# Attention probabilities transposed in 64x64 quarters inside the scoring visits of a three-block decoder layer

## The chip, the cores and the metric

The kernel runs on one core of a Trainium2 chip. The metric is the time of one execution on the device in microseconds; less is better. The engines of the core work side by side, each through a list of its own: TensorE (PE: matmuls, with PEld for the load of their stationary operand), VectorE (DVE), ScalarE (ACT), GpSimd (POOL), and SyncE (SP), which here only issues transfers. They meet through semaphores.

## The reference, cut to what matters

Everything is float32. x is (4, 256, 512), the context (4, 64, 512). Each of three blocks is followed by a residual and a layer norm:

```python
attn = einsum('ds,td->st', w1, w2) * sparse_mask          # block 1, 512x512
x = layernorm(x + gelu(einsum('bds,st->bdt', x, attn) + b2))
q = rope(x @ wq)          # block 2: 32 query heads of 128
k = rope(ctx @ wk); v = ctx @ wv                          # 8 key/value heads of 128, 64 keys
p = softmax(q @ k.T / sqrt(128) + mask)                   # per head and batch: 256 x 64
x = layernorm(x + (p @ v) @ wo)
x = layernorm(x + x @ W.T + b + lora(x, routing))         # block 3, 8 experts of rank 16
```

## The kernel before, in words

The tokens are 1024 rows, in 8 tiles of 128 (t = 0..7). A product that must keep float32 quality is made of three matmuls on operands that are split into a high and a low part (`mm3`, lines 261 to 263: high by high, low by high, high by low). ACT copies the high part out of PSUM (all its copies are line 801), DVE subtracts it to get the low part (all such subtractions are line 1139).

Block 2 is a loop over the 8 key/value heads g (`LAST` = 7). Group 0 is begun ahead of the hardware loop, which runs six times (g = 1..6), and group 7 is written out behind it. A group has four units u = 0..3: half u//2 of the tokens (tiles 4\*(u//2) to 4\*(u//2)+3) and a pair u%2 of its four query heads. For each unit:

- `query` (PE): two projections f = 0, 1 of 12 matmuls of 512 columns; ACT copies (`q_copy`), DVE and POOL rotate (`q_cos`, `q_sin`, `q_rot`).
- `scores`, or `score_pair` for two units at once (PE, line 369): the array is used as four quarters of 64x64; a quarter is plain float32, and each such matmul of the code is two MATMUL records in the trace.
- softmax: `mask_scores`, `row_max`, `shift` (DVE), `exps` (ACT), `row_sum`, `row_inverse` (DVE), `probs` (POOL, line 1728), which leaves the probabilities in SM, 128 tokens by 8 times 64.
- `probs_transpose` (PE, line 393): four 128x128 transposes of SM against the identity ID into one PSUM bank; `pt_hi` (ACT) and `pt_lo` (DVE) take them to PTh and PTl.
- `value_out(g, n)` (PE, n = 0..7): the values times a head's rows of wo, evicted by `vw_hi` and `vw_lo` to VWh and VWl; `attend(g, t)` (PE): six matmuls for a token tile, PT times VW, which `accumulate` (DVE) adds to the residual X, a step counted by the semaphore `x_added`.

The order of each engine's list is written out by hand; so are the PSUM banks (`T_BANKS` of the transposes, `A_BANKS` of attend, the last argument of `value_out`). A bank must have been read before PE writes it again, and this is why many waits on `x_added`, `vw_lo` and `pt_lo` stand in PE's list. After the loop the norm of block 2 needs an inverse root, found by a chain of 12 small dependent steps on POOL (`newton`, lines 1707 to 1713) behind DVE's `stats` and `guess`; ahead of the loop it is the same for block 1.

Of the kernel before, what the change touches and what calls it, by code (L numbers as in the profile page):

```python
# [9 lines left out]
F32R = mybir.dt.float32r  # L10
# [21 lines left out]
def decoder_layer(nc, x, ctx_in, amask, w1, w2, b2, smask, wq, wk, wv, wo, fW, fb, fA, fB, rW, rb, rope, out):  # L32
# [24 lines left out]
    with ExitStack() as es:  # L57
# [24 lines left out]
        PTh, PTl = (sb(f"PT{s}", [P, 2, B * S], F32R) for s in "hl")  # L82
# [26 lines left out]
        T_BANKS, A_BANKS = (7, 6, 7, 6), (6, 3, 6, 6, 6, 6, 3, 6)  # L109
# [49 lines left out]
        def x2_bank(t):  # L159
            return (5, 4, 3, 4, 3, 5, 3, 5)[t]  # L160
# [18 lines left out]

        def s_tiles(u):  # L180
            at = u % 2 * 4 * KS
            return bank[:, S_BANK:S_BANK + 2, at:at + 4 * KS].rearrange("p a (t k) -> p a t k", k=KS)

        def fy_bank(t):
            return (0, 6, 2, 7, 1, 3, 6, 7)[t]
# [8 lines left out]
        F_BANKS = (3, 0, 2, 1, 2, 1, 2)  # L194
        LORA_BANKS, ROUTE_BANK = (4, 3), 5
        TR_BANKS, W2_BANKS, AT_BANK = (6, 7, 0, 1, 6, 7, 0, 1, 6, 7, 6, 7, 6, 7, 6, 7, 6, 7), (0, 1, 6, 7), 2
        X_AT = (0, 1, 2, 3, 5, 7, 8, 9)
        X1_AT = (10, 11, 12, 13, 14, 15, 16, 17)
# [59 lines left out]
        def _(pe):  # L258
# [58 lines left out]
            def dense(t):  # L317
# [4 lines left out]
                pe.matmul(o, PTh[:, 1, 0:P], PTh[:, 0, 0:D], start=True, stop=False)  # L322
# [12 lines left out]
            def keys(g):  # L335
                pe.wait_ge(sm["wkv_lo"], 2 * g + 1)
                if isinstance(g, int) and g == 0:
                    pe.wait_ge(sm["tr_lo"], 7)
                project(k_out(g), 0).then_inc(sm["k_mm"], 1)

            def values(g):
                pe.wait_ge(sm["wkv_lo"], 2 * g + 2)
                if isinstance(g, int) and g == 0:
                    pe.wait_ge(sm["tr_lo"], 7)
                project(v_out(g), 1).then_inc(sm["v_mm"], 1)
# [59 lines left out]
            def attend(g, t):  # L405
# [5 lines left out]
                for pair in range(2):  # L411
                    m = mm3(bank[:, A_BANKS[t], :], PTh[:, pair, t * P:(t + 1) * P], PTl[:, pair, t * P:(t + 1) * P],
# [36 lines left out]
            def lora_out(t):  # L449
                pe.wait_ge(sm["ts_lo"], t // 4 + 1)  # L450
                pe.wait_ge(sm["f_lo"], 6)
                mm3(bank[:, fy_bank(t), :], PTh[:, 0, t * P:(t + 1) * P], PTl[:, 0, t * P:(t + 1) * P],
# [20 lines left out]
            w2_transpose(3)  # L473
            attn_chunk(1)
            pe.wait_ge(sm["w2t_lo"], 3)
            x_tile(0, 0)
            pe.wait_ge(sm["w2t_lo"], 4)
# [3 lines left out]
            attn_chunk(2)  # L481
            attn_last(0)
            attn_last(1)
            attn_last(2)
            pe.wait_ge(sm["w2t_lo"], 2)
            x_tile(3, 3)
            attn_last(3)
            pe.wait_ge(sm["tr_lo"], 1)
            ctx_tile(0, 4)
            pe.wait_ge(sm["tr_lo"], 2)  # L490
            x_tile(4, 5)
            pe.wait_ge(sm["tr_lo"], 3)
            ctx_tile(1, 6)
            pe.wait_ge(sm["tr_lo"], 4)
            x_tile(5, 7)
            pe.wait_ge(sm["at_masked"], 1)
            dense(0)
            pe.wait_ge(sm["at_masked"], 2)
# [30 lines left out]
            query(0, 0, 0)  # L529
            pe.wait_ge(sm["tr_lo"], 14)  # L530
            value_out(0, 0, 7)
            pe.wait_ge(sm["x_added"], 7)
            query(0, 0, 1)
            pe.wait_ge(sm["tr_lo"], 13)
            x1_tile(4, 14)
            pe.wait_ge(sm["x_added"], 8)
            value_out(0, 1, 3)
            pe.wait_ge(sm["vw_lo"], n_vw(0, 0))
            x1_tile(5, 15)
# [4 lines left out]
            pe.wait_ge(sm["at_masked"], 3)  # L544
            pe.wait_ge(sm["at_masked"], 4)
            scores(0, 0)
            pe.wait_ge(sm["tr_lo"], 15)
            x1_tile(6, 16)
            pe.wait_ge(sm["tr_lo"], 16)
            x1_tile(7, 17)  # L550
            pe.wait_ge(sm["q_rot"], n_rot(0, 0, 1))
            query(0, 1, 1)
            pe.wait_ge(sm["k_cos"], 1 + 1)
            query(0, 2, 0)
            pe.wait_ge(sm["tr_lo"], 18)
            value_out(0, 2, 7)
            pe.wait_ge(sm["vw_lo"], n_vw(0, 1))
            value_out(0, 3, 3)
# [3 lines left out]
            probs_transpose(0, 0)  # L562
            pe.wait_ge(sm["q_rot"], n_rot(0, 1, 0))
            query(0, 3, 0)
            pe.wait_ge(sm["vw_lo"], n_vw(0, 3))
# [3 lines left out]
            pe.wait_ge(sm["s_sub"], n_unit(0, 0))  # L569
            scores(0, 1)  # L570
            pe.wait_ge(sm["pt_lo"], n_unit(0, 0))
            value_out(0, 5, 7)

            with pe.Fori(1, LAST) as g:
                pe.wait_ge(sm["k_cos"], g + 1)
                query(g, 0, 0)
                pe.wait_ge(sm["s_sub"], n_unit(g - 1, 1))
                score_pair(g - 1, 3)
                pe.wait_ge(sm["q_rot"], n_rot(g - 1, 3, 0))
                values(g)  # L580
                pe.wait_ge(sm["x_added"], n_added(g - 2, 7))
                probs_transpose(g - 1, 1)
                pe.wait_ge(sm["vw_lo"], n_vw(g - 1, 4))
                value_out(g - 1, 6, 3)
                pe.wait_ge(sm["q_rot"], n_rot(g - 1, 3, 1))
                query(g, 0, 1)
                pe.wait_ge(sm["pt_lo"], n_unit(g - 1, 1))
                attend(g - 1, 0)
                pe.wait_ge(sm["vw_lo"], n_vw(g - 1, 5))
                value_out(g - 1, 7, 7)  # L590
                pe.wait_ge(sm["vw_lo"], n_vw(g - 1, 6))
                attend(g - 1, 1)
# [3 lines left out]
                probs_transpose(g - 1, 2)  # L596
                pe.wait_ge(sm["q_rot"], n_rot(g, 0, 1))
                query(g, 1, 1)
                pe.wait_ge(sm["pt_lo"], n_unit(g - 1, 2))
                value_out(g, 0, 7)  # L600
                pe.wait_ge(sm["x_added"], n_added(g - 1, 0))
                attend(g - 1, 2)
# [3 lines left out]
                attend(g - 1, 3)  # L606
                pe.wait_ge(sm["s_sub"], n_unit(g - 1, 3))
                score_pair(g, 1)
                pe.wait_ge(sm["x_added"], n_added(g - 1, 3))
                probs_transpose(g - 1, 3)  # L610
                pe.wait_ge(sm["x_added"], n_added(g - 1, 1))
                value_out(g, 1, 3)
                pe.wait_ge(sm["q_rot"], n_rot(g, 1, 1))
                query(g, 2, 1)
                pe.wait_ge(sm["pt_lo"], n_unit(g - 1, 3))
                attend(g - 1, 4)
                pe.wait_ge(sm["q_rot"], n_rot(g, 1, 0))
                query(g, 3, 0)
                pe.wait_ge(sm["vw_lo"], n_vw(g, 0))
                value_out(g, 2, 7)  # L620
                pe.wait_ge(sm["q_rot"], n_rot(g, 2, 0))
                keys(g + 1)
                pe.wait_ge(sm["vw_lo"], n_vw(g, 1))
                value_out(g, 3, 3)
                pe.wait_ge(sm["x_added"], n_added(g - 1, 4))
                attend(g - 1, 5)
                pe.wait_ge(sm["vw_lo"], n_vw(g, 2))
                probs_transpose(g, 0)
                pe.wait_ge(sm["q_rot"], n_rot(g, 2, 1))
                query(g, 3, 1)  # L630
                pe.wait_ge(sm["vw_lo"], n_vw(g, 3))
                attend(g - 1, 6)
                pe.wait_ge(sm["x_added"], n_added(g - 1, 5))
                attend(g - 1, 7)
                pe.wait_ge(sm["x_added"], n_added(g - 1, 6))
                value_out(g, 4, 3)
                pe.wait_ge(sm["pt_lo"], n_unit(g, 0))
                value_out(g, 5, 7)

            pe.wait_ge(sm["k_cos"], LAST + 1)  # L640
            query(LAST, 0, 0)
            pe.wait_ge(sm["vw_lo"], n_vw(LAST - 1, 4))
            value_out(LAST - 1, 6, 3)
            pe.wait_ge(sm["x_added"], n_added(5, 7))
            probs_transpose(LAST - 1, 1)
# [1257 lines left out]
```

## Time and profile before

| what | value |
|---|---|
| time, median of 3 runs | 492.2 us (491.89 to 492.32) |
| profiled execution, time | 492.99 us |
| its span, first to last instruction | 491.2 us |
| PE busy | 473.9 us, 96% |
| DVE / ACT / POOL busy | 408.3 / 260.6 / 273.4 us |
| mean granted clock of TensorE | 0.985 |

The span is what the trace shows; the profiled execution's own time is 1.8 us longer, for what lies around it. Matmuls overlap, so the share of PE is no measure of its speed, but a stretch in which PE never waits is one in which only less or cheaper PE work, or more clock, makes the kernel shorter.

### The profile page before, as it was taken

The numbers are of one execution on the slowest core, as the hardware profiler recorded it, in microseconds if no ns is written. First come the engines' busy times: TensorE is split into PE (matmuls) and PEld (weight loads), VectorE is DVE, ScalarE is ACT, GpSimd is POOL, SyncE is SP. The second block draws the span as 40 slices with busy tenths as digits, with TensorE's granted clock in tenths as the row PEclk, the third lists the DMA queues.
The fourth block names the chain that finished last, engine by engine and source line by source line (L and its number), as shares of the span: only waits on it lengthen the run. The fifth ranks groups of instructions, "written<-read, shape, count | busy, mean of one in ns | idle before, by whom it ended". The sixth has DMA issues, their size and how long they took to land.

```text
span 491.2 us, 11126 instructions
## 1 busy us (share of the span) xinstructions
PE 473.9 (96%) x4189; PEld 395.9 (81%) x4189; DVE 408.3 (83%) x739; ACT 260.6 (53%) x462; POOL 273.4 (56%) x347
## 2 busy tenths in 40 slices
PE   8999999999999999999999999999999999879991
PEld 8888778888888888888888888888888788668781
DVE  2779898988987898798979987988799889988585
ACT  4574447735673566365735663575458254353423
POOL 3477637854674467456636672676366423156523
PEclk9999999999999999999999999999999999979996
DMA  8943300240023011402040212022002400000013
GB/s 274 353 146 93 124 1 1 87 130 1 2 85 128 0 22 63 128 0 80 7 127 0 85 34 94 0 85 85 0 0 87 67 1 2 1 0 2 0 40 133
DMA packets 29137, 31.56 MB, mean 64 GB/s; under 512 B 6321, under 2 KB 16817, under 8 KB 29114
## 3 DMA queue, kind: packets, MB, share of 16 engines
q1 hardware_dynamic: 29114, 31.25, 20.1%
q8 instruction: 15, 0.25, 0.2%
q14 instruction: 8, 0.07, 0.0%
HBM read 29.15 MB, written 2.10 MB: 64 GB/s over the span
## 4 chain that ended last, share of the span: by engine, by line
PE 77%; DVE 9%; SPq 4%; POOL 3%; issue 3%; DMA 2%; ACT 1%; ACTq 0%; POOLq 0%; DVEq 0%
PE bank L261 23%; PE bank L263 22%; PE bank L262 22%; PE bank L369 6%; PE bank L393 3%; SPq L205 2%; DMA WQr<-in_L_xattn_wq_dram 2%; DVE X L1223 1%; DVE BST L1187 1%; PE bank L267 1%; POOL NW L1711 1%; DVE VWl L1139 1%; POOL NW L1709 1%; POOL RS L1713 1%; POOL NW L1707 1%
## 5 line engine op out<-in xcount | busy, mean ns | idle before, releaser
L1722 POOL TENSOR_TENSOR QS<-QS,SIN 128x512 f32<-128x512 f32 x64 | 83.0, 1297 | 124.4 <-ACT QS L801 124.4
L261 PE MATMUL bank<-XTh,WQh 128*128 128x512 f32 x256 | 101.7, 397 | 0.7 <-DVE XTl L1139 0.7
L263 PE MATMUL bank<-XTh,WQl 128*128 128x512 f32 x256 | 100.0, 391 | 0.0
L262 PE MATMUL bank<-XTl,WQh 128*128 128x512 f32 x256 | 99.7, 390 | 0.0
L1139 DVE TENSOR_TENSOR VWl<-bank,VWh 64x512 fp32r<-64x512 f32 x128 | 88.0, 688 | 9.3 <-ACT VWh L801 7.4
L801 ACT ACTIVATE QS<-bank 128x512 f32<-128x512 f32 x64 | 38.3, 598 | 103.1 <-PE bank L263 102.6
L801 ACT ACTIVATE VWh<-bank 64x512 fp32r<-64x512 f32 x128 | 75.9, 593 | 23.5 <-PE bank L263 20.9
L1251 DVE TENSOR_TENSOR bank<-bank,COS 128x512 f32<-128x512 f32 x64 | 44.6, 697 | 23.2 <-ACT QS L801 22.6
L261 PEld LDWEIGHTS bank<-XTh,WQh 128*128 128x128 f32 x256 | 48.1, 188 | 11.5 <-issue 1.3
L263 PEld LDWEIGHTS bank<-XTh,WQl 128*128 128x128 f32 x256 | 48.0, 188 | 10.5
L262 PEld LDWEIGHTS bank<-XTl,WQh 128*128 128x128 f32 x256 | 48.1, 188 | 9.5
L261 PE MATMUL bank<-VWh,PTh 128*128 128x512 f32 x128 | 50.9, 398 | 0.4 <-DVE X L1314 0.3
L262 PE MATMUL bank<-VWl,PTh 128*128 128x512 f32 x128 | 50.3, 393 | 0.0
L263 PE MATMUL bank<-VWh,PTl 128*128 128x512 f32 x128 | 50.1, 392 | 0.0
L1314 DVE TENSOR_TENSOR X<-X,bank 128x512 f32<-128x512 f32 x64 | 43.2, 674 | 7.2 <-PE bank L263 6.3
L1698 POOL TENSOR_TENSOR WOl<-WOr,WOh 128x512 fp32r<-128x512 f32 x32 | 41.3, 1291 | 12.1 <-ACT WOh L801 11.6
L1263 DVE TENSOR_TENSOR QR<-bank,QS 128x512 f32<-128x512 f32 x64 | 42.9, 683 | 0.4
L1688 POOL TENSOR_TENSOR WQl<-WQr,WQh 128x512 fp32r<-128x512 f32 x32 | 41.0, 1304 | 2.1 <-ACT WQh L801 2.1
L369 PEld LDWEIGHTS bank<-KK,QR 64*64 64x64 f32 x2048 | 31.6, 135 | 5.9 <-issue 5.8
L1728 POOL TENSOR_TENSOR SM<-SM,RI 128x512 f32<-128x512 f32 x32 | 33.5, 1046 | 3.8 <-DVE RI L1296 3.8
L369 PE MATMUL bank<-KK,QR 64*64 64x64 f32 x2048 | 34.2, 220 | 0.0
L261 PEld LDWEIGHTS bank<-VWh,PTh 128*128 128x128 f32 x128 | 24.3, 190 | 6.0 <-DVE X L1314 1.0
(150 smaller groups left out, 965.1 us busy)
## 6 DMA issues: line engine op xcount, KB each, us to landing
WQr<-in_L_xattn_wq_dram SPq DMA_DIRECT2D x8, 1024.0 KB, 5.5
WOr<-in_L_xattn_wo_dram SPq DMA_DIRECT2D x8, 1024.0 KB, 5.4
KVr<-in_L_xattn_wk_dram SPq DMA_DIRECT2D x8, 256.0 KB, 5.4
KVr<-in_L_xattn_wv_dram SPq DMA_DIRECT2D x8, 256.0 KB, 5.5
out_dram<-X SPq DMA_DIRECT2D x8, 256.0 KB, 2.0
X<-in_x_dram SPq DMA_DIRECT2D x3, 512.0 KB, 9.9
WQr<-in_L_attn_w_dram SPq DMA_DIRECT2D x4, 256.0 KB, 4.9
WOr<-in_L_attn_w_dram SPq DMA_DIRECT2D x4, 256.0 KB, 5.1
```

Of the source, the lines that this page charges most:

```text
L261: pe.matmul(o, lh, rh, start=start, stop=False)
L262: pe.matmul(o, lh, rl, start=False, stop=False)
L263: return pe.matmul(o, ll, rh, start=False, stop=stop)
L369: m = pe.matmul(s_tiles(u)[part, a, t, :], QR[head, u % 2, f, t * P + part.start:t * P + part.stop], KK[head, b, f, :], start=f == 0, stop ...
L801: return act.activation(o, i, ACT.Copy)
L1139: return dve.tensor_tensor(o, i, f32(hi), ALU.subtract)
L1251: dve.tensor_tensor(q, q, by_pos(COS, 2, S), ALU.mult).then_inc(sm["q_cos"], 1)
L1263: dve.tensor_tensor(QR[:, u % 2, f, :], bank[:, q_bank(u, f), :], QS[:, u % 2, 1 - f, :], ALU.add if f else ALU.subtract).then_inc(sm["q_r ...
L1314: dve.tensor_tensor(X[:, t, :], X[:, t, :], bank[:, A_BANKS[t], :], ALU.add)\
L1688: pool.tensor_tensor(wq_split(WQl, h), wq_head(WQr, h), f32(wq_split(WQh, h)), ALU.subtract)\
L1698: pool.tensor_tensor(WOl[:, h, :], WOr[:, h, :], f32(WOh[:, h, :]), ALU.subtract)\
L1722: pool.tensor_tensor(q, q, SIN[:, :].unsqueeze(1).broadcast_to([P, 2, S]), ALU.mult)\
```

## The change

1. `score_pair`, the visit that scores two units, first transposes the probabilities of the two units before them: `pair_transposes` issues 32 matmuls of 64x64 quarters (four for each 128x128 block of SM, each a plain float32 matmul of a piece of SM with a 64x64 piece of the identity) into the banks 6 and 7. `probs_transpose` stays only for the last two units of group 6 and the four of group 7.
2. One ACT copy (`pt_hi_pair`) and one DVE subtraction (`pt_lo_pair`) of 1024 columns over both banks take the place of two of each of 512. PTh and PTl are laid out anew for it (half, pair, 512).
3. `score_pair` now waits for the probabilities of both units (`p_done`) and for both banks, ahead of the scoring too.
4. The lists of all engines are written in another order, in all three stages, and many banks are others. One `value_out` of a group (n = 5) goes from the end of a loop pass to the start of the next.

```diff
+            def pair_transposes():
+                for n in range(8):
+                    for q in range(4):
+                        r, key = slice(64 * (q % 2), 64 * (q % 2) + 64), slice(64 * (q // 2), 64 * (q // 2) + 64)
+                        m = pe.matmul(t_quads()[key, q % 2, n, :], SM[r, n // 4, n % 4 * P + key.start:n % 4 * P + key.stop], ID[r, r],
+                                      start=True, stop=True)
+                return m
...
             def score_pair(g, u):
+                pe.wait_ge(sm["p_done"], UNITS * g + u - 1)
                 pe.wait_ge(sm["q_rot"], 2 * UNITS * g + 2 * u + 2)
...
                 pe.sem_inc(sm["s_begun"], 1)
+                pair_transposes().then_inc(sm["t_mm"], 2)
                 unit_scores(u - 1)
                 unit_scores(u).then_inc(sm["s_mm"], 2)
...
+            def pt_hi_pair(g, u):
+                act.wait_ge(sm["t_mm"], UNITS * g + u + 1)
+                if counted(g):
+                    act.wait_ge(sm["x_added"], n_added(g - 1, 2 * u + 1))
+                copy(pt_quads(PTh, u // 2), t_quads()).then_inc(sm["pt_hi"], 2)
...
+            def pt_lo_pair(g, u):
+                dve.wait_ge(sm["pt_hi"], UNITS * g + u + 1)
+                lo_part(pt_quads(PTl, u // 2), t_quads(), pt_quads(PTh, u // 2)).then_inc(sm["pt_lo"], 2)
...
-        T_BANKS, A_BANKS = (7, 6, 7, 6), (6, 3, 6, 6, 6, 6, 3, 6)
+        T_BANK = 6
+        T_BANKS, A_BANKS = (7, 7, 7, 7), (7, 6, 6, 7, 6, 3, 7, 6)
```

PE, in the loop, at the scoring visit of units 0 and 1 of group g. Before, the quarters of the scores stand alone, and a transposing visit (ID, SM) follows:

```order
L369 MATMUL bank<-KK,QR 64x64 x64
L609 REGISTER_ALU
L393 MATMUL bank<-ID,SM 128x128 x4
L611 REGISTER_ALU
L261 MATMUL bank<-WOh,VTh 128x512
```

After, at the same visit:

```order
L388 MATMUL bank<-ID,SM 64x64 x32
L379 MATMUL bank<-KK,QR 64x64 x64
L632 REGISTER_ALU
L271 MATMUL bank<-WOh,VTh 128x512
L272 MATMUL bank<-WOl,VTh 128x512
```

The transposes went from behind the scores to ahead of them, became 32 quarters for two units, and one such entry serves where two x4 entries were in a loop pass.

DVE, in the loop, behind the scoring visit of units 2 and 3 of the group before (KK,QR of PE). Before:

```order
L1280 TENSOR_REDUCE MX<-bank 128x8
L1275 SCALAR_TENSOR_TENSOR bank<-bank,MSK 128x2x256
L1285 REGISTER_ALU
L1287 TENSOR_TENSOR SM<-bank,MX 128x2x4x64
L1299 REGISTER_ALU
L1139 TENSOR_TENSOR PTl<-bank,PTh 128x512
```

After:

```order
L1290 SCALAR_TENSOR_TENSOR bank<-bank,MSK 128x2x256
L1294 REGISTER_ALU
L1295 TENSOR_REDUCE MX<-bank 128x8
L1154 TENSOR_TENSOR PTl<-bank,PTh 128x2x8x64
L1278 TENSOR_TENSOR QR<-bank,QS 128x512
```

The subtraction for PTl is one of twice the size, third behind the mask and the maximum of unit 2.

POOL, behind the loop, where group 7 ends. Before, the end of the first Newton chain, its shift, the last unit's `probs` and the first `add_bias`:

```order
L1711 TENSOR_SCALAR NW<-NW 128x2
L1713 TENSOR_TENSOR RS<-RS,NW 128x2
L1758 TENSOR_TENSOR NM<-MV,RS 128x2
L1760 TENSOR_SCALAR NM<-NM 128x2
L1728 TENSOR_TENSOR SM<-SM,RI 128x512
L1765 TENSOR_TENSOR X<-X,WOr 128x512 x2
```

After, the `probs` of the last units and the begin of that chain:

```order
L1738 TENSOR_TENSOR QS<-QS,SIN 128x512 x2
L1744 TENSOR_TENSOR SM<-SM,RI 128x512 x2
L1723 TENSOR_TENSOR NW<-RS 128x2
L1725 TENSOR_TENSOR NW<-NW,VH 128x2
L1727 TENSOR_SCALAR NW<-NW 128x2
```

The last unit's `probs` stood behind the whole chain and its shift, and now stands ahead of it.

## Rows read from the trace of the kernel before

**Rows 1.** The page's head: the span, and the busy time of each engine.

```profile
span 491.2 us, 11126 instructions
PE 473.9 (96%) x4189; PEld 395.9 (81%) x4189; DVE 408.3 (83%) x739; ACT 260.6 (53%) x462; POOL 273.4 (56%) x347
```

**Rows 2.** Windows: length, then PE, PEld, DVE, ACT, POOL busy; clock, DMA, GB/s.

```profile
228.10:275.40 47.30, 47.30 (x466) 39.72 (x465) 40.48 (x67) 26.60 (x49) 28.41 (x25) 1.00 0.18 55
370.00:437.00 67.00, 62.59 (x652) 51.80 (x650) 61.19 (x110) 34.73 (x62) 27.25 (x36) 0.97 0.12 29
```

**Rows 3.** The page's chain that ended last, by engine.

```profile
PE 77%; DVE 9%; SPq 4%; POOL 3%; issue 3%; DMA 2%; ACT 1%; ACTq 0%; POOLq 0%; DVEq 0%
```

**Rows 4.** Timeline of PE: first query of loop, of group 7, last matmul.

```profile
86.34 0.39 PE L261 MATMUL bank<-XTh,WQh 128*128 128x512 f32 x1
...
370.03 0.39 PE L261 MATMUL bank<-XTh,WQh 128*128 128x512 f32 x1
...
480.65 0.39 PE L263 MATMUL bank<-WOh,PTl 128*128 128x512 f32 x1
```

**Rows 5.** Groups of PE by form: records, busy us, mean ns.

```profile
L369 PE MATMUL bank<-KK,QR 64*64 64x64 f32 x2048 | 34.2, 220 | 0.0
L393 PE MATMUL bank<-ID,SM 128*128 128x128 f32 x128 | 19.9, 280 | 2.3 <-POOL SM L1728 2.3
L282 PE MATMUL bank<-ID 128*128 128x128 f32 x24 | 4.7, 371 | 1.5 <-POOL ID L1769 1.5
```

**Rows 6.** Timeline of PE around one transposing visit of the loop.

```profile
220.65 0.39 PE L263 MATMUL bank<-VWh,PTl 128*128 128x512 f32 x1
220.88 0.60 PE L393 MATMUL bank<-ID,SM 128*128 128x128 f32 x4
221.23 0.48 PE L261 MATMUL bank<-XTh,WQh 128*128 128x512 f32 x1
221.55 0.40 PE L262 MATMUL bank<-XTl,WQh 128*128 128x512 f32 x1
```

**Rows 7.** Timeline of PE: a scoring visit of one unit, one of two.

```profile
84.45 1.16 PE L369 MATMUL bank<-KK,QR 64*64 64x64 f32 x64
85.54 0.50 PE L261 MATMUL bank<-WOh,VTh 128*128 128x512 f32 x1
...
230.98 2.10 PE L369 MATMUL bank<-KK,QR 64*64 64x64 f32 x128
233.00 0.39 PE L261 MATMUL bank<-CTh,KVh 128*128 128x256 f32 x1
```

**Rows 8.** Timeline of DVE in the loop: PTl; mask and maximum behind the scores.

```profile
223.31 0.68 DVE L1139 TENSOR_TENSOR PTl<-bank,PTh 128x512 fp32r<-128x512 f32 x1
...
233.14 0.70 DVE L1275 SCALAR_TENSOR_TENSOR bank<-bank,MSK 128x512 f32<-128x512 f32 x1 [0.36 <-PE bank L369]
233.87 0.69 DVE L1280 TENSOR_REDUCE MX<-bank 128x8 f32<-128x512 f32 x1
```

**Rows 9.** Timeline of ACT in the loop: a copy of 1024 columns.

```profile
234.86 1.06 ACT L801 ACTIVATE KVh<-KVr 128x1024 fp32r<-128x1024 f32 x1
```

**Rows 10.** Timeline of PE ahead of the loop: the longest wait there.

```profile
53.30 0.47 PE L261 MATMUL bank<-XTh,WQh 128*128 128x512 f32 x1 [0.65 <-DVE XTl L1139]
```

**Rows 11.** Timeline of PE in group 7: its two long waits.

```profile
429.93 0.50 PE L261 MATMUL bank<-WOh,VTh 128*128 128x512 f32 x1 [1.69 <-DVE VWl L1139]
...
433.63 1.08 PE L393 MATMUL bank<-ID,SM 128*128 128x128 f32 x4 [2.30 <-POOL SM L1728]
```

**Rows 12.** Timeline of POOL in group 7: first step of the chain, last `probs`.

```profile
428.53 0.19 POOL L1707 TENSOR_TENSOR NW<-RS 128x2 f32<-128x2 f32 x1 [8.15 <-DVE RS L1203]
...
432.44 1.04 POOL L1728 TENSOR_TENSOR SM<-SM,RI 128x512 f32<-128x512 f32 x1
```

**Rows 13.** Windows of 5 us in group 7, columns as in Rows 2.

```profile
430.00:435.00 5.00, 2.70 (x14) 2.31 (x15) 4.84 (x10) 4.13 (x8) 2.75 (x10) 0.74 0.00 0
435.00:440.00 5.00, 5.00 (x20) 4.38 (x19) 3.21 (x7) 2.14 (x4) 2.51 (x2) 0.58 0.00 0
```

More of the change, by code:

```diff
@@ L605, in _ @@
                 pe.wait_ge(sm["x_added"], n_added(g - 1, 2))
[L606 to L612, printed above, removed]
+                value_out(g, 1, 6)
+                pe.wait_ge(sm["vw_lo"], n_vw(g, 0))
+                value_out(g, 2, 3)
@@ L679, in _ @@
+            query(LAST, 2, 1)
+            pe.wait_ge(sm["pt_lo"], n_unit(LAST - 1, 3))
             probs_transpose(LAST, 0)
-            pe.wait_ge(sm["vw_lo"], n_vw(LAST, 0))
-            value_out(LAST, 1, 3)
-            pe.wait_ge(sm["x_added"], n_added(LAST - 1, 3))
+            pe.wait_ge(sm["q_rot"], n_rot(LAST, 1, 0))
+            weight_transpose(1)
+            pe.wait_ge(sm["vw_lo"], n_vw(LAST, 1))
             attend(LAST - 1, 4)
+            pe.wait_ge(sm["f_lo"], 1)
+            attend(LAST - 1, 5)
@@ L720, in _ @@
+            pe.wait_ge(sm["x_added"], n_added(LAST - 1, 7))
+            attend(LAST, 1)
+            pe.wait_ge(sm["x_added"], n_added(LAST, 1))
+            attend(LAST, 2)
+            pe.wait_ge(sm["x_added"], n_added(LAST, 0))
+            probs_transpose(LAST, 2)
+            pe.wait_ge(sm["q_rot"], n_rot(LAST, 2, 0))
+            weight_transpose(3)
+            pe.wait_ge(sm["vw_lo"], n_vw(LAST, 4))
+            value_out(LAST, 5, 3)
             pe.wait_ge(sm["x_added"], n_added(LAST, 2))
+            value_out(LAST, 6, 6)
@@ new lines, in _ @@
+            pe.wait_ge(sm["vw_lo"], n_vw(LAST, 6))
+            attend(LAST, 4)
+            pe.wait_ge(sm["vw_lo"], n_vw(LAST, 7))
+            attend(LAST, 5)
+            pe.wait_ge(sm["pt_lo"], n_unit(LAST, 3))
+            attend(LAST, 6)
+            pe.wait_ge(sm["x_added"], n_added(LAST, 4))
+            attend(LAST, 7)
+            pe.wait_ge(sm["tr_lo"], 19)
+            x2_tile(1)
+            pe.wait_ge(sm["f_lo"], 4)
+            base(0)
+            pe.wait_ge(sm["s_sub"], n_unit(LAST, 3))
@@ L1551, in _ @@
+            vw_lo(LAST - 1, 7, 3)
+            q_cos(LAST, 0, 1)
+            v_lo(LAST)
+            q_rot(LAST, 0, 0)
             mask_scores(LAST - 1, 2)
+            pt_lo_pair(LAST - 1, 1)
+            q_rot(LAST, 0, 1)
             row_max(LAST - 1, 2)
@@ L1579, in _ @@
+            q_rot(LAST, 1, 1)
+            row_max(LAST, 0)
+            accumulate(LAST - 1, 3)
+            vw_lo(LAST, 0, 3)
+            shift(LAST, 0)
+            q_cos(LAST, 2, 0)
+            row_sum(LAST, 0)
+            pt_lo(LAST - 1, 3)
             row_inverse(LAST, 0)
-            q_rot(LAST, 1, 1)
-            vw_lo(LAST, 0, 3)
-            q_cos(LAST, 2, 0)
+            vw_lo(LAST, 1, 6)
             mask_scores(LAST, 1)
             row_max(LAST, 1)
+            shift(LAST, 1)
@@ L1625, in _ @@
-            f_lo(2)
-            row_inverse(LAST, 3)
-            vw_lo(LAST, 6, 3)
+            accumulate(LAST - 1, 6)
+            q_rot(LAST, 3, 0)
+            accumulate(LAST - 1, 7)
+            q_rot(LAST, 3, 1)
+            f_lo(2)
+            accumulate(LAST, 0)
+            stats(1, 0)
+            mask_scores(LAST, 3)
+            row_max(LAST, 3)
+            vw_lo(LAST, 4, 3)
+            accumulate(LAST, 1)
+            shift(LAST, 3)
+            stats(1, 1)
+            row_sum(LAST, 3)
@@ L1628, in _ @@
+            accumulate(LAST, 2)
+            row_inverse(LAST, 3)
+            pt_lo(LAST, 2)
+            guess(1, 0)
+            f_lo(3)
+            vw_lo(LAST, 5, 3)
+            accumulate(LAST, 3)
+            vw_lo(LAST, 6, 6)
             stats(1, 2)
[L1629 to L1630 removed]
             pt_lo(LAST, 3)
+            stats(1, 3)
+            vw_lo(LAST, 7, 3)
+            guess(1, 1)
             x2_lo(0)
[L1633 removed]
             accumulate(LAST, 4)
[L1635 removed]
```

819 lines of the change are left out of this document (378 added, 441 removed).

## The prediction

> **What bounds the kernel now.** I read the page's head and the chain first. PE is busy for 96% of the span [rows 1], and 77% of the chain that ended last is PE [rows 3]. The share says little while matmuls overlap, so I looked at where PE waits. A window of one loop pass is 47.30 us long with PE busy for all 47.30 and the clock at 1.00 [rows 2]: in the loop PE never waits. There only the price of PE's own work counts, and any delay of another engine is free up to its slack. The window of group 7 has 62.6 of 67.0 us busy and a clock of 0.97 [rows 2]: here waits and the clock decide, and DVE, busy for 61.2, sets them. From the first query of the loop to the first query of group 7 there are (370.03 - 86.34)/6 = 47.28 us a pass; ahead of the loop lie 86.3 us, behind it 121.1 us, of which PE works until about 480.9 [rows 4].
>
> **The transposes, the core of the change.** A transposing visit of PE stands between two matmuls that would follow each other at 0.23 us (220.65 to 220.88). From 220.65 to 221.55 are 0.90 us with one visit and two such steps, so the visit costs 0.44 us [rows 6], and two units 0.88.
>
> The new one is 32 matmuls of 64x64 quarters in plain float32. The program scores with 1024 such matmuls (32 for each of 32 units) and the trace has 2048 records of them; the 12 plain matmuls of the warming have 24 [rows 5]. The transposes that go have one record each, 128 for 32 units times 4 [rows 5]. So the 32 new matmuls are 64 records, not 32, and this decides the sum. A visit of 64 records takes 1.09 us until the next matmul, one of 128 takes 2.02 [rows 7]: 64 more records in a visit that is there anyway cost 0.93 us. They have the form of the scores (64 rows, 64 columns, the four quarters in turn, row halves to different banks), so I take 0.93; half of 2.02, 1.01, is the upper end, 0.46 the lower, if the trace's doubling did not hold here.
>
> A pair thus costs 0.93 for 0.88: +0.05. Against this stands that the matmuls right behind a lone transposing visit start a little apart (0.32 us for the first step, 0.23 otherwise, in [rows 6]), a few hundredths of which the 0.44 may miss. A pass has two pairs, and I take its PE work as unchanged, 47.28 us; from -0.15 to +0.25 a pass, which is -0.9 to +1.5 for six.
>
> A rule that speaks against the change: the Trainium skill (TensorEngine Tiling (Array Packing), Feature Incompatibilities) says that tiling by columns excludes the transpose mode for float32 inputs, and TensorE: Matmul & The Clock Gate (Terms) calls that mode four times faster for float32. By the whole of that factor the price of the eight blocks, 0.88 us, would be 3.5, halved for 64 instead of 128 columns 1.8 us a pair. By the row it is 0.93, since the scores already are plain quarters; the doubled records agree with the rule's direction, not with its size.
>
> **Evictions in the loop.** Two copies and two subtractions of 512 columns become one each of 1024. ACT has a copy of 1024 at 1.06 us [rows 9]. DVE's of 512 is 0.68 alone [rows 8] and follows another at about 0.6, so I take 1.25 for the pair (2 x 0.60 to 2 x 0.68). What counts is whether they are there in time, since nothing else waits on PE in a pass. Behind the visit of units 2 and 3, `pt_lo_pair` is third on DVE: the mask starts 0.14 after the visit (233.00, 233.14), the maximum 0.73 after the mask [rows 7, 8], the subtraction 0.6 later, and it ends 2.7 us behind the visit. PE has a query (12 x 0.227 = 2.7) and a `value_out` (0.7) to do, 3.4 us, ahead of `attend`, and wants the weights some 0.2 sooner. Slack 0.45 us. Behind the other visit it is one rotation (0.6), the mask (0.7) and the pair (1.25), again 2.7 against 3.4. The copy is ahead of both, since the transposes now stand ahead of the scores and end about 2 us before them. The probabilities are wanted ahead of the visit: POOL ends those of unit 1 about 1.2 us early, those of unit 3 about 0.8. So the loop has no wait, cost 0.
>
> **Ahead of the loop.** One `value_out` (3 x 0.23 = 0.68 us) and the visit of unit (0, 0), 0.44, leave it: -1.1. Its waits: now there is 0.8 us at 53.30 (52.49 to 53.30, of which the row calls 0.65 idle) [rows 10] and some 0.7 in two short ones. In the new order `x_tile(7)` waits for the copy and split of `x1_tile(1)`, which stands on DVE behind `normalize(0, 2)` and so behind the second Newton chain on POOL; the first chain is now behind one more subtraction of 1.3 us. I get PE ready at 45.1 and the tile at 46.6, a wait of 1.5, and 0.5 at the last quarter of `dense(0)`. New 2.0 for old 1.5: in sum -0.6, between -1.3 and +0.6.
>
> **Behind the loop.** The `value_out` comes here (+0.68), the pair of group 6 costs 0.93 for a 0.44 visit (+0.5). Before, PE waits 1.69 and 2.30 us [rows 11] and about 0.7 elsewhere. The second is there because the last `probs` stands behind the Newton chain and shift on POOL, from 428.53 to 432.44 [rows 12]. Then the clock falls to its half level, 1.2 GHz: windows at 0.74 and 0.58 make (0.26 + 0.42) x 5/0.5 = 6.8 us of it [rows 13], some 5.6 of them with PE at work, so 2.8 us lost. The transposes at 433.63 take 1.08 for 0.60 [rows 11, 6]. Together 7.5 us.
>
> After: `probs(7, 3)` stands ahead of the chain and that wait is gone, but others come. (a) `attend(7, 2)` follows `attend(7, 1)` in the same bank and waits for its `accumulate`, on DVE behind a mask, a maximum and a `vw_lo`: 1.9 us. (b) The transposes of (7, 3) wait for `accumulate(7, 3)`: 1.8. (c) `x2_tile(0)` waits for the first `normalize`, ACT behind the same 3.9 us of POOL chain and behind `vw_hi(7, 7)`: 1.7. (d) `attend(7, 4)` waits for the last `vw_lo`: 0.7. Together 6.2 us with the clock full: -1.3. At the very end POOL's last chains set the pace; `guess(2, 1)` comes some 0.6 us earlier against PE's end, so does the end: -0.7. The stage: +0.7 +0.5 -1.3 -0.7 = -0.8; with my walk's ends -2.5 to +1.0 at full clock.
>
> **Sum.** -0.6 + 0 - 0.8 = -1.4 us in the span of 491.2 [rows 1], 489.8. The profiled execution took 492.99 for it, the median of the runs 492.2; I apply the difference to the median: 490.8.
>
> **The rivals.**
> 1. *The clock halves again behind the loop.* For it: waits (b), (c), (d) stand within 7 us, 4.2 idle, while before 4.0 idle within 6 us went with the fall [rows 11, 13]; the total of the waits is larger. Against: single waits are shorter, the longest 1.9 for 2.30. PE then has some 5 us of bound work at half speed: +2.6, 493.4.
> 2. *The loop waits for the pair* (slower). DVE's list is full, and one subtraction of twice the size holds what is behind it. If `pt_lo_pair` ends over 0.45 us later than worked out, PE waits in each of six passes; at 1.2 us late in one place 6 x 0.75 = 4.5 us, 495.3. It decides from 0.6 us late on. Against: all durations are from rows, and there is no wait in the passes of before.
> 3. *The quarters are as dear as the rule on the transpose mode says*: 1.8 for 0.93 in 13 pairs, +11, 502. Against: 2048 records of that form at 0.93 for 64 [rows 5, 7].
> 4. *Better than summed*: the quarters are single records (0.46 each pair, 13 x -0.47 = -6, 484.7), or, likelier, waits (a) to (c) overlap with one another and the tail saves 3: 488.
> 5. *Nothing gained or lost*: the DVE and ACT time saved lies where PE never waits, and waits only change places. This is my sum without the tail's two gains, 492.
>
> **How the numbers follow.** Forecast 490.8 with 0.38 (its own range 489.7 to 492). Rival 1 0.25, rival 2 0.10, rival 3 0.03, rival 4 0.15, rival 5 0.09. A measurement of this kernel tells about 0.2%, 1.0 us, from no change. Below 491.2: 0.26 of the forecast's 0.38, all of 4, a little of 5: 0.43. Above 493.2: most of 1, 2 and 3: 0.28. Between: 0.29. The range leaves out 4's single records, the far side of 2, and 3: 487.8 to 494.6.
>
> **What the changed profile would show.** Right: 64 records of ID,SM quarters a pair at 14 to 16 ns apart; a pass between 47.1 and 47.5 us with PE busy throughout; the two 1024-column evictions at about 1.06 and 1.25 us; PE's first long wait at `x_tile(7)`; behind the loop waits at the second `attend` of group 7, at the last transposes, at the first `x2_tile`; no or a shorter window below clock 1.00 before PE's end. Wrong: a wait of PE for PTl in the passes (rival 2), 32 records or another spacing (3, 4), a window near 0.6 around the last transposes (1). If the stage ahead of the loop or behind it differs from my sum by over 1 us, the order was misread, not the price of the quarters.

## The result, and the profile after

| | before | after |
|---|---|---|
| median of runs, one chip | 492.26 us (491.89 to 493.34, 4 runs) | 497.77 us (497.05 to 498.36, 4 runs) |
| ratio, 95% interval | | 1.0107 (1.0092 to 1.0121) |
| span of the profiled execution | 491.2 us | 495.9 us |
| first query of the loop | 86.34 | 86.69 |
| one loop pass | 47.28 | 47.37 |
| first query of group 7 to the end | 121.2 | 125.0 |

The changed kernel is slower by 5.5 us, forecast was 1.4 less. Run again on another chip it took 498.01 us for 492.33, ratio 1.0099 (1.0084 to 1.0113). The spans differ by 4.7 us only, since the profiled execution of before was 0.7 above its median. One execution of experiment 9 (1215.81 us) is counted as slow and stays out of its ratio. The page's head, to be held against [rows 1]:

```profile
span 495.9 us, 12575 instructions
PE 474.7 (96%) x4917; PEld 397.1 (80%) x4917; DVE 411.7 (83%) x726; ACT 260.2 (52%) x449; POOL 272.6 (55%) x347
```

Windows of a loop pass and of two stretches of group 7, against [rows 2, 13], columns as there:

```profile
228.80:276.17 47.37, 47.37 (x577) 40.03 (x576) 40.21 (x65) 26.54 (x47) 28.29 (x25) 1.00 0.18 55
425.00:430.00 5.00, 2.94 (x13) 2.06 (x12) 4.82 (x10) 1.82 (x3) 0.00 (x0) 0.96 0.00 0
430.00:435.00 5.00, 5.00 (x21) 4.24 (x20) 3.38 (x11) 2.55 (x5) 1.94 (x6) 0.70 0.00 0
```

The reader sees again a pass without a wait, with 111 more records, and a stretch of 3.4 us at the half clock, (0.04 + 0.30) x 5/0.5, where before had 6.8. A pair's visit in the loop, timeline of PE, and the two evictions, of ACT and DVE:

```profile
237.52 0.39 PE L273 MATMUL bank<-XTh,WQl 128*128 128x512 f32 x1
237.84 1.16 PE L388 MATMUL bank<-ID,SM 64*64 64x64 f32 x64
238.82 2.05 PE L379 MATMUL bank<-KK,QR 64*64 64x64 f32 x128
240.80 0.50 PE L271 MATMUL bank<-XTh,WQh 128*128 128x512 f32 x1
...
239.78 1.02 ACT L813 ACTIVATE PTh<-bank 128x1024 fp32r<-128x1024 f32 x1
...
242.28 1.22 DVE L1154 TENSOR_TENSOR PTl<-bank,PTh 128x1024 fp32r<-128x1024 f32 x1
```

64 records and 0.98 us until the scores. The subtraction ends at 243.50, 2.7 us behind the visit as worked out. PE's list waits for it ahead of `attend`, whose first matmul starts at 244.34, so 0.84 us were to spare. All rows of the view of PE's waits (columns: us in total, times, longest):

```profile
PE bank L271 <- DVE X L1333: 2.1, 1, 2.1
PE bank L277 <- ACT X L944: 2.0, 2, 1.8
PE bank L277 <- DVE XTl L1154: 1.8, 1, 1.8
PE bank L292 <- POOL ID L1785: 1.5, 1, 1.5
PE bank L379 <- issue: 1.4, 1, 1.4
PE bank L414 <- DVE X L1333: 1.4, 1, 1.4
PE bank L271 <- DVE VWl L1154: 1.1, 2, 0.6
```

`x_tile`, `x1_tile` and `x2_tile` are the transposes of a token tile for blocks 1, 2 and 3, and `dense` is block 1's product. Five waits were forecast by place, and come within half a microsecond of their size: `x_tile(7)` ahead of the loop (1.5 forecast, 1.8), the second `attend` of group 7 (1.9, 2.1), the last transposes (1.8, 1.4), the first `x2_tile` (1.7, 1.8), `attend(7,4)` (0.7, 0.5). The row of ID stands in before too [rows 5]. One row, `issue`, is no wait for an engine and was not forecast. Timeline of PE at the only pair visit behind the loop:

```profile
379.93 1.16 PE L388 MATMUL bank<-ID,SM 64*64 64x64 f32 x64
380.91 1.79 PE L379 MATMUL bank<-KK,QR 64*64 64x64 f32 x107
384.13 0.57 PE L379 MATMUL bank<-KK,QR 64*64 64x64 f32 x21 [1.42 <-issue]
384.63 0.50 PE L271 MATMUL bank<-XTh,WQh 128*128 128x512 f32 x1
```

In the middle of the scores, with no semaphore between them, PE stands still for 1.42 us. The scores take 3.72 us (380.91 to 384.63) where in the loop they take 1.98, so the place costs 1.74. In the DMA view the queue of kind "instruction" has packets of 16 KB. Its rows for 130:369 (five passes, no q8) and for 380.5:383 (queue, kind: packets, MB, share):

```profile
q1 hardware_dynamic: 9504, 12.58, 16.6%
q14 instruction: 1, 0.01, 0.0%
...
q8 instruction: 1, 0.02, 2.4%
```

From 125.0 to 381.3 no packet of q8 comes, and the first one falls into this visit. Before has the same picture: none from 127 to 375.4, the first at 375.5, inside a visit with only 128 quarter records (373.96 to 375.99), and there PE does not stop.

**Where the span's 4.7 us are.** Ahead of the loop +0.35. The loop 6 x 0.09 = +0.55. Behind it +3.8. For this last part I added up in both traces what each step of PE takes over its plain cadence (0.227 us for a matmul of 512 columns, 0.119 for 256, 0.0155 for a quarter's record, 0.057 for a 128x128 transpose). The moved `value_out` is +0.68, the pair for a single visit +0.54, the stop in the scores +1.74, the other steps up to the scores of unit (7, 3) -0.6; from there to the four last `attend` 9.9 us over cadence for 9.0, +0.9; in block 3, where `x2_tile` now stands singly, 3.9 for 2.9, +1.0; the end behind PE's last matmul -0.5 (10.04 for 10.55 us).

### The profile page after: what moved, and what is told of

Its sections match the earlier page's. It is cut to its first block, busy times and chain, and to the rows that moved or that the text cites. A ratio compares the mean times of both kernels' runs of the same rounds, so it can differ in the third digit from the quotient of the medians.

```text
span 495.9 us, 12575 instructions
## 1 busy us (share of the span) xinstructions
PE 474.7 (96%) x4917; PEld 397.1 (80%) x4917; DVE 411.7 (83%) x726; ACT 260.2 (52%) x449; POOL 272.6 (55%) x347
## 4 chain that ended last, share of the span: by engine, by line
PE 84%; DVE 8%; POOL 3%; ACT 3%; issue 2%; POOLq 0%; ACTq 0%; DVEq 0%
PE bank L271 24%; PE bank L273 23%; PE bank L272 23%; PE bank L379 6%; PE bank L388 3%; DVE BST L1202 1%; PE bank L277 1%; DVE VWl L1154 1%; PE bank L292 1%; DVE X L1333 1%; DVE VE L1211 1%; POOL NW L1727 1%; ACT VWh L813 1%; POOL NW L1723 1%; DVE X L1238 1%
## 5 line engine op out<-in xcount | busy, mean ns | idle before, releaser
L909 ACT ACTIVATE SM<-SM 128x512 f32<-128x512 f32 x32 | 20.2, 631 | 43.6 <-DVE SM L1302 43.4
```

## The experiments

Times are medians beside the kernel before on the same chip (492.3 to 492.6 us in all); 497.8 and 498.0 are the changed kernel (ratios 1.0107 and 1.0099). Chips differ a little, so two versions on different chips are better compared by their ratios to the kernel before. The order of the first four follows one question: what is the stop inside the scores, and what does a pair cost?

**1. Whole transposes in the pair behind the loop (e1_whole_tail).**

In `score_pair`, where g is a number and not the loop's register (behind the loop), with evictions to match:

```diff
+            def whole_transposes():
+
+                for n in range(8):
+                    m = pe.transpose(bank[:, T_BANK + n // 4, n % 4 * P:(n % 4 + 1) * P], SM[:, n // 4, n % 4 * P:(n % 4 + 1) * P], ID[:, :])
+                return m
...
-                pair_transposes().then_inc(sm["t_mm"], 2)
+                (whole_transposes if isinstance(g, int) else pair_transposes)().then_inc(sm["t_mm"], 2)
```

> The changed kernel, but the one pair visit behind the loop (group 6, units 2 and 3) transposes with 8 whole 128x128 transposes, one record each, and not with 64 quarter records; the loop is untouched. Theory 'code supply': the gap of 1.42 us inside the scores of that visit is PE waiting for its own code, because 192 short records follow each other just where code has to be fetched again for the first time after the loop. With 136 records instead, the first fetch falls late in the scores, a long query follows, and the gap is gone: the visit (380.91 to 384.63 for the scores, 3.72 us) falls to about 2.0, the time by 1.5 to 1.8 us. Rival 'the pair itself' (the wait for both units, the banks, a transfer beside it): the gap stays at 1.2 to 1.6 us, the time changes by 0.1 or less.

495.88 us, ratio 1.0070 (1.0057 to 1.0084): 1.9 to 2.1 less than the changed kernel, 1.4 to 1.8 by the ratios. Timeline of PE at the visit:

```profile
379.39 1.04 PE L386 MATMUL bank<-ID,SM 128*128 128x128 f32 x8
380.36 2.10 PE L379 MATMUL bank<-KK,QR 64*64 64x64 f32 x128
382.38 0.50 PE L271 MATMUL bank<-XTh,WQh 128*128 128x512 f32 x1
```

The stop is gone and the scores take 2.02. From the first query of group 7 to PE's last matmul are 113.06 us (370.48 to 483.54) for 114.93.

**2. The stop made in the kernel before (e4_before_dense).**

In `score_pair` of the kernel before, again where g is a number:

```diff
+                if isinstance(g, int):
+                    unit_scores(u - 1)
                 unit_scores(u - 1)
                 unit_scores(u).then_inc(sm["s_mm"], 2)
```

> The kernel before with one thing added: in the double scoring visit behind the loop (group 6) the scores of one unit are issued twice (64 more quarter records, same result), so that the visit has 192 quarter records as the changed kernel has. Theory 'code supply': besides their own 0.99 us they bring a gap of about 1.0 to 1.7 us into that visit, in sum 2.0 to 2.7 us more. Rival 'the pair itself': 1.0 us more and no gap.

494.12 us, 1.0033 (1.0021 to 1.0045), so 1.5 more. Timeline of PE, the last of 192 quarter records (the first starts at 373.99) and what follows:

```profile
377.89 0.56 PE L369 MATMUL bank<-KK,QR 64*64 64x64 f32 x19 [1.12 <-issue]
378.38 0.38 PE L261 MATMUL bank<-CTh,KVh 128*128 128x256 f32 x1
```

The stop is there, without pair, new banks or new order. The scores take 4.39 us for 2.03, 2.4 more, as expected. The last transposes are 1.9 us late, and 0.9 of it came back since 3.4 us of group 7 then lay at the half clock for 6.8, which the expectation had left out. The rival (1.0 us and no stop) is refuted.

**3. The pair of the loop issued twice (e3_twice_loop).**

```diff
                 pe.sem_inc(sm["s_begun"], 1)
+                if not isinstance(g, int):
+                    pair_transposes()
                 pair_transposes().then_inc(sm["t_mm"], 2)
```

> The changed kernel with the pair transposes of the loop issued twice, the second time over the first (same result), so 12 more visits of 64 records. If a loop pass has no wait and a pair costs what its records show (0.98 us), a pass grows by 1.96 us and the time by 11.8. If the records hide a price or a slack is used up (evictions come 1 us later against the work that wants them only if that is ahead of the scores, so this is not expected), more than 13. If the pair overlaps with something, under 10.

511.66 us, 1.0396 (1.0380 to 1.0412): 13.9 more than the first measurement of the changed kernel, not 11.8. A pass from the second on is 49.24 us, 1.87 more for two pairs of visits: 0.93 each. The first pass is 2.7 us longer than the others (51.97). Timeline of PE in that pass:

```profile
97.95 2.03 PE L379 MATMUL bank<-KK,QR 64*64 64x64 f32 x123
101.34 0.34 PE L379 MATMUL bank<-KK,QR 64*64 64x64 f32 x5 [1.37 <-issue]
...
122.11 0.68 PE L379 MATMUL bank<-KK,QR 64*64 64x64 f32 x33
123.54 1.62 PE L379 MATMUL bank<-KK,QR 64*64 64x64 f32 x95 [0.75 <-issue]
```

So the stop comes with runs of many short records in code that runs for the first time, in the first pass and behind the loop (0.97 us here), and in none of the five repeated passes, though they have the same visits. That is what the supply of code would do, and nothing else proposed would. One thing more speaks for it: in all ten stops of the eight profiles that have one, PE goes on 2.2 to 2.7 us after a 16 KB packet of q8 has started (381.7 and 384.13 in the changed kernel, 375.5 and 377.89 in experiment 2). Not each such run stops, though: the changed kernel's first pass has two visits of 192 records (scores at 96.70 and 118.25), each with a packet of q8 in it, and no stop. What decides this, no run shows.

**4. All pairs whole (e2_whole_all).** The edit of 1 for every g.

> The changed kernel with all 13 pair visits made of 8 whole transposes. Theory 'priced by the row': an x8 visit of the kernel before takes 0.97 us until the scores behind it, the quarters take 0.98, and the step ahead of quarters is 0.32 for 0.23: 0.1 us less a pair, so a loop pass of 47.37 becomes about 47.17 and the loop 1.2 us shorter, with the 1.6 us behind the loop together 2.8 us less. Rival 'quarters are dear' (1.8 us a pair): over 10 us less. Rival 'quarters are free': a pass stays at 47.37 or gets longer.

497.0 us, 1.0084 (1.0071 to 1.0098), where 2.8 us less than the changed kernel, 495.0, was expected; the runs lie from 493.76 at a mean clock of 0.995 to 497.22 at 0.986, so the median says little. The profile decides the loop: a pass is 47.26, 0.12 less than with quarters and 0.02 less than before. A pair of quarters costs 0.06 us more than 8 whole transposes (0.1 was expected). They are neither dear nor free.

**5. The joined eviction split again (e5_split_evict).**

```diff
-                copy(pt_quads(PTh, u // 2), t_quads()).then_inc(sm["pt_hi"], 2)
+                for a in range(2):
+                    copy(w_unit(PTh, u // 2, a), t_unit(a)).then_inc(sm["pt_hi"], 1)
...
-                lo_part(pt_quads(PTl, u // 2), t_quads(), pt_quads(PTh, u // 2)).then_inc(sm["pt_lo"], 2)
+                for a in range(2):
+                    lo_part(w_unit(PTl, u // 2, a), t_unit(a), w_unit(PTh, u // 2, a)).then_inc(sm["pt_lo"], 1)
```

> The changed kernel, but each pair is evicted in two copies and two subtractions of 512 columns again (same banks, same quarters, same places in the lists of ScalarE and VectorE). A copy of 512 takes 0.60 us and two follow at about 0.5 to 0.6, so 1.1 for 1.02; two subtractions 1.3 for 1.22. Theory 'TensorE sets the loop': a pass stays at 47.37 us and the time at that of the changed kernel within 0.3 us; the joined eviction brought nothing. Rival 'VectorE's list is at its edge in the loop': each pair comes 0.1 to 0.2 us later and passes grow, by 1 us or more in all.

498.39 us, 1.0119 (1.0105 to 1.0134), 0.4 to 0.6 more (0.6 to 1.0 by the ratios). A pass is 47.37 us as in the changed kernel: in the loop the join brings nothing, as theory had it. The profiled execution was the longest of the five, 501.28 us, and its time went elsewhere. Timeline of PE ahead of the loop:

```profile
48.37 0.98 PE L283 MATMUL bank<-ID,X 128*128 128x128 f32 x4 [1.80 <-DVE XTl L1161]
49.00 0.78 PE L338 MATMUL bank<-PTh 128*128 128x512 f32 x1
49.57 0.63 PE L277 MATMUL bank<-VWh,XTh 128*128 128x512 f32 x1
```

Windows of the same kernel there:

```profile
45.00:50.00 5.00, 3.20 (x21) 2.81 (x19) 4.40 (x8) 1.75 (x5) 2.91 (x6) 0.86 0.20 59
50.00:55.00 5.00, 5.00 (x23) 4.16 (x22) 2.84 (x7) 3.39 (x7) 3.89 (x12) 0.80 0.47 181
```

Behind the same wait for `x_tile(7)`, 1.80 us, the granted clock is at its half level for (0.14 + 0.20) x 5/0.5 = 3.4 us, and the loop begins at 88.7 for 86.7. Group 7 of this profile has two more such stretches. What the other four executions lost, no trace shows.

**6. One wait behind the loop mended (e6_drain_swap, e7_bank0).** The first:

```diff
             row_max(LAST, 3)
-            vw_lo(LAST, 4, 3)
             accumulate(LAST, 1)
+            vw_lo(LAST, 4, 3)
```

> The changed kernel with two neighbours in VectorE's list of group 7 exchanged: accumulate of tile 1 stands ahead of the vw_lo of value_out 4. The second attend of group 7 waits 2.06 us for that accumulate (425.8 to 428.6). Theory 'each wait is one entry in a list': the wait shrinks by the 1.4 us of vw_lo, and what comes behind wants nothing earlier, so the time falls by 0.7 to 1.4 us, up to 3 if the clock does not fall behind the shorter wait. Rival 'VectorE as a whole sets the drain': the next wait grows by as much, and the time changes by less than 0.3.

498.11 us, 1.0108 (1.0095 to 1.0121): no gain. The profiled run was the longest, 498.93 us, and its clock fell ahead of the loop too (as in 5). Behind the loop its PE needs 114.12 us for 114.93. Rows of PE's waits in timeline form:

```profile
429.37 0.50 PE L271 MATMUL bank<-VWh,PTh 128*128 128x512 f32 x1 [0.78 <-DVE X L1333]
433.37 0.50 PE L271 MATMUL bank<-WOh,VTh 128*128 128x512 f32 x1 [0.78 <-DVE X L1333]
437.84 1.12 PE L414 MATMUL bank<-ID,SM 128*128 128x128 f32 x4 [2.12 <-DVE X L1333]
```

The wait went from 2.06 to 0.78; a new one of 0.78 stands at a `value_out`, and the next grew from 1.39 to 2.12. The second gives the last transposes bank 0:

```diff
-            pe.wait_ge(sm["x_added"], n_added(LAST, 3))
+            pe.wait_ge(sm["f_lo"], 4)
             probs_transpose(LAST, 3)
```

> The changed kernel with the transposes of the last unit of group 7 written to bank 0 and not 7, so that they wait for the weight split that last read bank 0 and not for the accumulate of tile 3 (1.39 us at 437.00). They should stand at 435.5. Theory 'each wait is one entry in a list': the last value_out then starts at 436.3 for 437.4, the copy of the probabilities and the first normalize on ScalarE come 1.1 to 1.5 us earlier, the wait at the first x2_tile goes from 440.5 to about 439.3, and the time falls by about 1.1. Rival 'VectorE as a whole sets the drain': under 0.3.

497.73 us, 1.0113 (1.0088 to 1.0138): nothing. The steps came where they were forecast, `value_out` at 436.28 and `x2_tile` at 439.46, and yet:

```profile
436.28 0.50 PE L274 MATMUL bank<-WOh,VTh 128*128 128x512 f32 x1 [0.21 <-DVE VWl L1157]
439.46 0.63 PE L280 MATMUL bank<-ID,X 128*128 128x128 f32 x4 [1.77 <-ACT X L947]
442.17 0.47 PE L274 MATMUL bank<-VWh,PTh 128*128 128x512 f32 x1 [1.64 <-DVE VWl L1157]
```

`attend(7,4)` starts at 442.17 with the mend and without it: 1.1 us less wait became 1.1 us more in the wait for the last `vw_lo`, which stands where it stood in VectorE's list.

**7. The wait ahead of the loop mended (e9_dense_ahead).**

```diff
+            pe.wait_ge(sm["x_added"], 5)
+            dense(6)
             pe.wait_ge(sm["tr_lo"], 11)
             x_tile(7, 11)
-            pe.wait_ge(sm["x_added"], 5)
-            dense(6)
```

> The changed kernel with dense(6) ahead of x_tile(7) on TensorE, ahead of the loop, nothing else. x_tile(7) waits 1.79 us for the split of x1_tile(1), and dense(6), 3.1 us of matmuls, is ready at 44.4. Theory 'the prologue's cost is this one wait': the wait goes, some 0.5 to 0.8 come back at x1_tile(3), which shares the bank of x_tile(7); the loop begins 0.9 to 1.3 us earlier, at 85.4 to 85.8, and the clock cannot fall there: 0.9 to 1.3 us less than the changed kernel, more against runs in which its clock fell. Rival 'DVE's and POOL's chain of the norm sets it': the wait moves to dense(7) or to the first query and the time changes by less than 0.3.

498.15 us, 1.0109 (1.0093 to 1.0126), beside 498.01 of the changed kernel on the same chip. The rival was right:

```profile
51.04 0.66 PE L277 MATMUL bank<-ID,X 128*128 128x128 f32 x4 [0.98 <-DVE XTl L1154]
55.49 0.47 PE L271 MATMUL bank<-XTh,WQh 128*128 128x512 f32 x1 [0.80 <-DVE XTl L1154]
```

The 1.79 us came back as 0.98 at `x1_tile(3)` and 0.80 at the first query, which waits for a split behind the same norm. Beside it ran the changed kernel itself:

> The changed kernel as it is, beside the next ones on one chip, since the kernels measured so far shared none with it. Expected: 497.8 us (497.0 to 498.5) if the clock stays full ahead of the loop as in its first profile; up to 1.5 us more in those runs in which it halves at the wait for x_tile(7), as it did in two profiles of kernels that differ from this one only behind that place.

498.01 us (496.18 to 498.19); in its profile the clock is full at `x_tile(7)`.

**8. Three mends together (e10_three_mends).** The edits of 1, of 6 (the exchange) and of 7.

> The changed kernel with three of its costs mended together: whole transposes in the one pair behind the loop (1.9 us less alone), the accumulate ahead of vw_lo in group 7 (0.8 less behind the loop by its profile), dense(6) ahead of x_tile(7) (about 1 less). If they add up: 494.1 us, 493.5 to 494.8, and it is still slower than the kernel before by 1.5 us, for what is left are the 0.09 us of each loop pass, the value_out that went behind the loop, and waits of block 3. If one drain absorbs another's gain, 495 to 496.

496.28 us, 1.0079 (1.0066 to 1.0093): 1.7 less than the changed kernel beside it, 1.0 by the ratios. That is no more than the gain of experiment 1 alone; the other two add nothing, as 6 and 7 showed by themselves.

**9. A version of the kernel before (c1_before_probs, c1_again).** The same look at lists, turned on the kernel before, whose 2.30 us wait [rows 11] stands behind POOL's chain [rows 12]:

```diff
-            newton(1, 0)
+            newton(1, 0, lambda: probs(LAST, 3))
             mean_shift(1, 0)
-            probs(LAST, 3)
```

`newton` issues the probs ahead of the last of its three rounds. On VectorE `row_inverse(LAST, 3)` goes ahead of `f_lo(2)` and `pt_lo(LAST, 3)` ahead of the last `vw_lo`, on ScalarE `pt_hi(LAST, 3)` ahead of `normalize(1, 0)`, on TensorE `weight_transpose(4)` ahead of `x2_tile(0)`.

> The kernel before with the drain of group 7 set in another order, nothing else: the last probs stands ahead of the third round of the first Newton chain on POOL, row_inverse ahead of a weight's subtraction on VectorE, the copy and the subtraction of the last probabilities ahead of the two normalize and of the last vw_lo, and a weight transpose ahead of the first two x2_tile on TensorE. By the rows of before the last transposes stand at 432.1 for 433.6 and the last four attend start at 435.5 for 436.9. Theory 'each wait is one entry in a list': the time falls by 1 to 1.5 us, up to 3 if less of the work lies at the half clock. Rival 'VectorE as a whole sets the drain': under 0.5, since it is busy without a gap from 428.5 to 437.9.

491.67 us for 492.50, 0.9987 (0.9975 to 0.9999). Again on another chip:

> The kernel before with the drain of group 7 in another order, once more, on another chip and beside the others: 0.8 us less than the kernel before (0.3 to 1.3), with a mean clock of 0.99 or above where that of before is 0.985, if what was measured first is the order and not the chip.

492.24 for 492.33, 0.9989 (0.9980 to 0.9998). By the ratios it is 0.5 to 0.6 us faster, both times, and each interval ends just short of 1; that is below the 0.2% that a measurement of this kernel can tell, so it may be nothing, and it is less than the 1 us or more that was expected. The second time the medians differ by 0.1 us where 0.8 was expected, and the mean clocks are 0.985 to 0.995, not all 0.99 or above. Timeline of PE in the first profile (the clock is 1.00 here; at 0.58 to 0.74 in [rows 13]):

```profile
432.58 0.63 PE L393 MATMUL bank<-ID,SM 128*128 128x128 f32 x4 [0.82 <-POOL SM L1730]
433.04 0.60 PE L426 MATMUL bank<-ID,WOr 128*128 128x128 f32 x4
435.09 1.34 PE L267 MATMUL bank<-ID,X 128*128 128x128 f32 x8 [1.44 <-ACT X L926]
```

The wait of 2.30 us became one of 0.82 and a new one of 1.44, and the four last `attend` start 65.9 us behind the first query of group 7 for 66.9. It is the only version whose median was below both kernels'.

## Why the prediction was wrong, by its own steps

**The price of the quarters was right in the loop.** 64 records, 0.93 us for a further visit (experiment 3: 1.87 for two), 0.98 in place; a pair costs 0.05 more than two single visits, a pass 0.09 more, forecast 0.10 as two times +0.05 and then rounded away in "I take its PE work as unchanged": 0.55 us in the sum. Rival 3, worked out from the Trainium skill's rule on the transpose mode (TensorEngine Tiling (Array Packing), Feature Incompatibilities), is refuted in its size: whole transposes in all pairs save 0.06 us a pair, not 0.9.

**Evictions in the loop: right.** 1.02 and 1.22 us, no wait in any pass, and split again they cost a pass nothing (experiment 5). Behind this visit 0.84 us were left, 0.6 with the prediction's 0.2 for the weights, where it gave 0.45. Rival 2 is out. It also means that the change's saving on DVE and ACT in a pass (0.3 and 0.1 us busy by the windows) lies where nobody waits.

**Ahead of the loop: off by 1.0.** Forecast -0.6, found +0.35 in the profile, within the bounds of that stage (-1.3 to +0.6), as the loop's +0.55 is (-0.9 to +1.5). The place and size of the wait at `x_tile(7)` were right (1.5 for 1.8), that at `dense(0)` near (0.5 for 0.6). What failed is "new 2.0 for old 1.5": it counts two named waits, and by the sum over the cadence the new order has 1.3 us more, not 0.5. Experiment 7 shows why no single entry of PE's list sets this: the wait moves to the next tile of the norm. And a wait of 1.8 us for one of 0.65 brings a risk that the sum does not have: in 2 of 8 profiles of kernels with this order (experiments 5 and 6) the clock halved behind it, 2 us each, and in none of the four profiles with the old order did it halve there.

**Behind the loop: off by 4.6, the step that decided.** Forecast -0.8 with bounds of -2.5 to +1.0, found +3.8. Three things, against which small steps up to the scores of unit (7, 3) give 0.6 back:

- The stop inside the pair's scores, 1.74 us, was in no term and no rival. The prediction costed 64 more records by visits of the loop and of the group ahead of it, and carried that price to the one visit behind the loop, where code comes in for the first time. Experiments 1, 2 and 3 settle that it takes short records in code that is new: taken away, 1.4 to 2.1 us less; put into the kernel before, a stop of 1.12; doubled in the loop, stops in the first pass and in no later one. That it is the arrival of code is inferred from this and from the packets of q8. The Trainium skill (Runtime: NRT & Kernel Launch, Instruction fetch mechanics) says that an engine's instructions come in blocks of 16 KiB, fetched one ahead while the current one executes, and that a crossing is mostly hidden. The packets of 16 KB agree. "Mostly hidden" agrees with the traces where matmuls of 0.12 to 0.23 us follow, for no gap without a releaser stands there; it does not agree with the ten stops of 0.75 to 1.42 us among quarter records of 0.0155 us. The prediction closed with the rule that a stage off by over 1 us means a misread order and not the price of the quarters. For 1.74 of the 4.6 us here that rule was wrong: the quarters brought them, in the one place where the loop's price does not hold.
- The drain. Waits (a) to (d) were forecast as 6.2 (the four terms add up to 6.1) and are 5.8. But "with the clock full" failed: the clock was at half for 3.4 us, 1.7 of work lost. This is rival 1 in weaker form (2.6). The drain came to +0.9, where the forecast had -1.3. Both of its sums were low, as the 9.0 and 9.9 us over cadence show: "together 7.5 us" for before by 1.5, 6.2 for after by 3.7. The clock is 1.7 of the 3.7; what the rest is made of was not taken apart.
- Block 3, +1.0, was taken as unchanged. `x2_tile` visits stand singly there, and one of them waits 0.27 us for its tile (the other wait in that row of the list is (c)); no run tried this part.

The end behind PE was forecast at -0.7 and is -0.5, and the moved `value_out` and the pair at +0.68 and +0.5, found 0.68 and 0.54.

**The sum.** The span was missed by 1.0 + 0.5 + 4.6 = 6.1 us and the median by 7.0; the other 0.8 lies between the profiled executions and the medians, a difference that the prediction carried over as fixed. **The range** (487.8 to 494.6) would not have held the time even without the stop: 497.8 - 1.9 is 495.9, and experiment 1 measured 495.88. Nor with the clock full up to PE's end: one execution of the changed kernel had a mean clock of 0.995, at which the profile of experiment 8 shows the clock full up to PE's end, and took 496.18. Rival 5's 492 does not follow from its own sum either: 490.8 without the two gains of 1.3 and 0.7 is 492.8. The waits' places were read well and their sum was not, because each was priced as if it could be added: experiments 6 to 8 show the same from the other side, three forecasts of about 1 us for one mended wait, and none was paid out in the time.

**What stays open:** the 1.0 us of block 3 and what it would take to bring it back; and in which runs the clock falls. The same program ended at mean clocks of 0.982 to 0.995 and at 496.0 to 500.0 us (e7_bank0), so single medians near each other (experiments 4 and 6) rest on the profile more than on the time.

## What to carry to other kernels

A price read in a loop need not hold for code that runs once. Where many instructions of some 15 ns follow each other in such code, look in the trace for gaps with no releaser; here long matmul records in that place took the gap away. A wait on a full list of another engine is not a term that can be taken away singly: ask when the entry after the next one ends, since that is what PE meets next. And joining two evictions into one is worth nothing in a stage where the engines that evict are never waited for.

## What the runs showed of the hardware

- PE stopped for 0.75 to 1.42 us within a run of quarter matmuls, with nothing to wait for, in the first pass of the loop and behind the loop only (three kernels' profiles above; also the other profiles with the quarter pair behind the loop, 0.88 to 1.34).
- In these ten stops PE went on 2.2 to 2.7 us after a packet of the instruction queue q8 had started. Two visits of 192 quarter records in the changed kernel's first pass had a packet too, and no stop.
- The instruction queue q8 moved nothing from 125.0 to 381.3 us, while a loop with 577 matmul records a pass ran over five times.
- The same wait of 1.79 to 1.81 us was followed by 3.4 us at the half clock level in two profiles and by full clock in six.
- Plain float32 quarters transposed a pair of units in 0.98 us, 8 transposes of 128x128 in 0.97.
